# Start of a decoder kernel: order of the vector loads, of the first casts and of the passes of the first projection

## What is computed

```python
x = x + _L0_attn_ref(_layernorm(x, axis=-1), L0_attn_ln1_g, L0_attn_ln1_b,
                     L0_attn_Wq, L0_attn_bq, L0_attn_Wk, L0_attn_bk,
                     L0_attn_Wv, L0_attn_bv, L0_attn_Wg, L0_attn_bg, ...)
x = x + _L0_xattn_ref(_layernorm(x, axis=-1), ctx_1024, ...)
...
```

## Time and profile before

| | us |
|---|---|
| median of three runs | 1394.85 (1392.35 to 1399.29) |
| profiled execution, its own time | 1394.02 |
| its span | 1392.2 |
| PE, PEld, DVE, ACT, POOL busy in the span | 1247.0, 1071.0, 1004.3, 752.3, 251.1 |
| mean granted clock of PE | 0.963 |

### The profile page before, as it was taken

One profiled execution on the slowest core, in us unless ns is written; L12 is line 12 of the kernel. 1 busy time (PEld: TensorE's weight loads), 2 busy tenths in 40 slices (PEclk: granted clock), 3 DMA queues, 4 the chain that ended last, 5 costly groups with the idle time before them and its releaser, 6 DMA issues.

```text
span 1392.2 us, 27638 instructions
## 1 busy us (share of the span) xinstructions
PE 1247.0 (90%) x9826; PEld 1071.0 (77%) x9826; DVE 1004.3 (72%) x2479; ACT 752.3 (54%) x1781; POOL 251.1 (18%) x338
## 2 busy tenths in 40 slices
PE   5999999979999999999999999999888999979518
PEld 4889888868788777887778778787677777769518
DVE  5975776656667777777777777777777985676984
ACT  5653535335655555555555555555545764425862
POOL 2433333326000000000000000000034444110100
PEclk9999999989999999999999999999999999989859
DMA  9200101041000000000000000000020003310001
GB/s 286 67 1 5 43 1 46 0 155 48 1 12 12 12 13 11 0 12 11 12 11 11 1 11 12 11 0 1 1 61 2 3 2 114 103 30 0 1 0 48
DMA packets 34547, 40.65 MB, mean 29 GB/s; under 512 B 4889, under 2 KB 29066, under 8 KB 34442
## 3 DMA queue, kind: packets, MB, share of 16 engines
q1 hardware_dynamic: 33614, 39.24, 9.1%
q10 hardware_dynamic: 828, 0.14, 0.1%
HBM read 35.36 MB, written 4.01 MB: 28 GB/s over the span
## 4 chain that ended last, share of the span: by engine, by line
PE 50%; DVE 17%; issue 6%; ACT 4%; POOL 1%; DVEq 0%; DMA 0%; SPq 0%; ACTq 0%; POOLq 0%
PE bank L791 8%; PE bank L793 7%; PE bank L792 7%; PE bank L1014 4%; PE bank L1004 3%; PE bank L996 3%; PE bank L972 3%; ACT prob L1695 2%; DVE nmx L2375 2%; DVE amax L2574 2%; PE bank L1248 2%; DVE kTl L2146 2%; PE bank L1386 1%; PE bank L1266 1%; DVE prob L2392 1%
## 5 line engine op out<-in xcount | busy, mean ns | idle before, releaser
L1695 ACT ACTIVATE prob<-bank,nmx 100x361 f32<-100x361 f32 x256 | 142.5, 560 | 202.9 <-DVE nmx L2375 198.8
L2375 DVE TENSOR_REDUCE nmx<-bank 100x1 f32<-100x361 f32 x256 | 124.1, 526 | 62.6 <-PE bank L996 61.6
L695 POOL TENSOR_TENSOR frstd<-fmoments,eps 100x1 f32<-100x1 f32 x32 | 6.2, 194 | 645.0 <-DVE fmoments L2318 645.0
L791 PE MATMUL bank<-cxTh,wxkh 128*128 128x362 f32 x256 | 99.9, 390 | 9.3 <-DVE kTl L2146 8.2
L2392 DVE TENSOR_SCALAR prob<-prob,rsum 100x361 f32<-100x361 f32 x256 | 92.9, 405 | 4.5
L1004 PE MATMUL bank<-ident,prob 100*128 100x100 f32 (+1 forms) x768 | 89.6, 252 | 0.6 <-DVE prob L2392 0.5
L1004 PEld LDWEIGHTS bank<-ident,prob 100*128 100x128 f32 (+1 forms) x768 | 84.5, 151 | 6.2 <-DVE prob L2392 1.9
L791 PE MATMUL bank<-wxvh,cxTh 128*128 128x512 f32 (+1 forms) x192 | 84.4, 440 | 1.6 <-DVE vv L2298 1.2
L793 PE MATMUL bank<-cxTh,wxkl 128*128 128x362 f32 x256 | 84.1, 329 | 0.0
L792 PE MATMUL bank<-cxTl,wxkh 128*128 128x362 f32 x256 | 83.8, 327 | 0.0
L1014 PE MATMUL bank<-pT,vv 128*64 128x100 f32 (+1 forms) x1536 | 81.5, 255 | 1.7 <-ACT pT L1689 0.6
(11 more groups left out here) (432 smaller groups left out, 3703.6 us busy)
## 6 DMA issues: line engine op xcount, KB each, us to landing
cx<-in_ctx_dram SPq DMA_DIRECT2D x32, 128.0 KB, 2.1
xc<-in_ctx_dram SPq DMA_DIRECT2D x32, 128.0 KB
parked_weights<-parking SPq DMA_DIRECT2D x9, 256.0 KB, 5.6
mask_i<-in_mask_BxS_ik_dram SPq DMA_DIRECT2D x16, 141.0 KB
w<-in_L_attn_W_dram SPq DMA_DIRECT2D x2, 1024.0 KB, 13.5
cx<-in_ctx_dram SPq DMA_DIRECT2D x16, 105.0 KB, 2.0
xc<-in_ctx_dram SPq DMA_DIRECT2D x16, 105.0 KB
x<-in_x_dram SPq DMA_DIRECT2D x4, 400.0 KB
```

The costliest lines, as they stand in the source:

```text
L791: pe.matmul(o, wh, mh, start=start, stop=False)
L1695: nc.scalar.activation(prob[:, h % 4, :], bank[S_BANKS[e]][0:T, 0:S], ACT.Exp, bias=nmx[:, h:h + 1], accum_out=psum_[:, h:h + 1]).then_inc ...
L2375: nc.vector.tensor_reduce(nmx[:, h:h + 1], bank[S_BANKS[e]][0:T, 0:S], AX_X, ALU.max, negate=True).then_inc(xa_max, 1)
```

## The change

ACT no longer issues the last seven of the 15 vectors; SP does, right behind the first rows and ahead of the first weight. The four small tensors that are wanted late are issued by ACT after the two square roots, not before. A square root of one column (`warm`) is put right behind ACT's remaining issues, with no wait for the rows. The high parts of the first halves of Wk and Wg move from ACT to DVE (`tensor_copy`, followed by the subtraction), and DVE's waits for `l0_wh` drop by two. The low part of the rows for k = 1 of the first group moves from POOL to DVE, behind the low part of Wg. PE no longer waits for the low rows before `project(0)`: for K it runs the four passes without them as each k of the high rows is there, then waits for `l0_z` and runs the two passes with them.

```diff
--- before.py
+++ after.py
@@ -109,6 +109,7 @@
         decay = sb("decay", [P, KC])
         act_scale = sb("act_scale", [P, 4])
         pause = sb("pause", [1, 4])
+        warm = sb("warm", [P, 1])
         stats_all = sb("stats_all", [T, B, 6])
         moments_all = sb("moments_all", [T, B, 2])
         std_all = sb("std_all", [T, B])
@@ -383,6 +384,8 @@
         RELB_DMAS = 3 + 8
 
 
+        SP_VECTORS = 8
+
         def side_jobs():
 
             jobs = []
@@ -509,6 +512,11 @@
                 sp.dma_start(dst, a[name].rearrange("(k p) n -> p k n", p=P)).then_inc(count, 16)
 
             load_rows(0)
+            for name, n in VECTORS[SP_VECTORS:]:
+                r = COL[name]
+                src = (a[name].rearrange("(c h) d -> c (h d)", h=2) if name.startswith("L0_xattn")
+                       else a[name][0:n * P].rearrange("(c p) -> c p", p=P))
+                sp.dma_start(rows[r:r + n, :], src).then_inc(vec_in, 16)
             projections = (("L0_attn_Wk", wk0), ("L0_attn_Wg", wg0), ("L0_attn_Wv", wv0), ("L0_attn_Wq", wq0))
             for n, (name, dst) in enumerate(projections):
                 load_half(name, dst, 0, wa_in[n])
@@ -639,7 +647,7 @@
                 nc.gpsimd.tensor_tensor(el0[:, n % 2, :], full[:, n % 2, :], eh0[:, n % 2, :].bitcast(F32), ALU.subtract).then_inc(l0_es, 1)
 
             def rows_low0(g):
-                for k in range(KD):
+                for k in range(KD if g else 1):
                     pool.wait_ge(l0_y, KD * g + k + 1)
                     nc.gpsimd.tensor_tensor(rows_t[g % 2][1][:, k, :], y_rows[:, k, :], rows_t[g % 2][0][:, k, :].bitcast(F32), ALU.subtract).then_inc(l0_z, 1)
 
@@ -828,7 +836,7 @@
                 rows_h, rows_l = rows_t[n // KC % 2]
                 for kind in kinds:
                     high, low, b, free = KINDS[kind]
-                    if c == 0 and kind == 0:
+                    if c == 0 and kind == 0 and n:
                         pe.wait_ge(l0_z, KD * (n // KC) + KD)
                     if n == 0:
                         pe.wait_ge(l0_wl, kind + 1)
@@ -836,9 +844,18 @@
                         pe.wait_ge(l0_wb, kind + 1)
                     if n:
                         pe.wait_ge(free, n)
-                    for k in range(KD):
-                        mm = split_matmul(bank[b][:, 0:N], high[:, k, cols], low[:, k, cols], rows_h[:, k, :], rows_l[:, k, :],
-                                          k == 0, k == KD - 1)
+                    if n == 0 and kind == 0:
+                        for k in range(KD):
+                            pe.wait_ge(l0_y, k + 1)
+                            pe.matmul(bank[b][:, 0:N], high[:, k, cols], rows_h[:, k, :], start=(k == 0), stop=False)
+                            pe.matmul(bank[b][:, 0:N], low[:, k, cols], rows_h[:, k, :], start=False, stop=False)
+                        pe.wait_ge(l0_z, KD)
+                        for k in range(KD):
+                            mm = pe.matmul(bank[b][:, 0:N], high[:, k, cols], rows_l[:, k, :], start=False, stop=(k == KD - 1))
+                    else:
+                        for k in range(KD):
+                            mm = split_matmul(bank[b][:, 0:N], high[:, k, cols], low[:, k, cols], rows_h[:, k, :], rows_l[:, k, :],
+                                              k == 0, k == KD - 1)
                     mm.then_inc(l0_proj, 1)
 
             def summed(n, high, low, wh, wl, ready, count):
@@ -1469,19 +1486,14 @@
                 return vec[:, COL[name] + c:COL[name] + c + 1]
 
             act.dma_start(ident[:], a["identity"]).then_inc(vec_in, 16)
-            for name, n in VECTORS:
+            for name, n in VECTORS[:SP_VECTORS]:
                 r = COL[name]
                 src = (a[name].rearrange("(c h) d -> c (h d)", h=2) if name.startswith("L0_xattn")
                        else a[name][0:n * P].rearrange("(c p) -> c p", p=P))
                 act.dma_start(rows[r:r + n, :], src).then_inc(vec_in, 16)
             act.dma_start(logits[:], a["L0_attn_decay_logit"].rearrange("(c h) -> c h", h=2)).then_inc(vec_in, 16)
-            act.dma_start(delta[:, 0:KD * 8].rearrange("p (k n) -> p k n", k=KD),
-                          a["L0_ffn_delta_w"].rearrange("(k p) n -> p k n", p=P)).then_inc(small_in, 16)
-            act.dma_start(delta[:, KD * 8:], a["L0_ffn_delta_act"].partition_broadcast(P)).then_inc(small_in, 16)
-            act.dma_start(onehot[:], a["bucket_onehot"]).then_inc(small_in, 16)
-            act.dma_start(rel[0:BUCKETS, :], a["L1_attn_rel_emb"]).then_inc(small_in, 16)
-
             act.wait_ge(memsets, 2)
+            nc.scalar.activation(warm[:], eps[:], ACT.Sqrt)
             def rows_out(g, k, b):
                 nc.scalar.copy(zT[:, 2 * g:2 * g + 2, k, :], bank[b][:, 0:N].rearrange("d (a q) -> d a q", a=2)).then_inc(ln_done, 1)
 
@@ -1556,11 +1568,14 @@
                 nc.scalar.copy(cxTh[:, buf, k, 0:S], src[:, 0:S]).then_inc(xa_ch, 1)
 
             first_deviations(1, 0, 1)
+            act.dma_start(delta[:, 0:KD * 8].rearrange("p (k n) -> p k n", k=KD),
+                          a["L0_ffn_delta_w"].rearrange("(k p) n -> p k n", p=P)).then_inc(small_in, 16)
+            act.dma_start(delta[:, KD * 8:], a["L0_ffn_delta_act"].partition_broadcast(P)).then_inc(small_in, 16)
+            act.dma_start(onehot[:], a["bucket_onehot"]).then_inc(small_in, 16)
+            act.dma_start(rel[0:BUCKETS, :], a["L1_attn_rel_emb"]).then_inc(small_in, 16)
             act.wait_ge(prep_vec, 1)
             nc.scalar.mul(vecs[:], bank[SIDE_BANK0][:, 0:NV], DH ** -0.5)
             nc.scalar.copy(vec[:], bank[SIDE_BANK0][:, 0:NV]).then_inc(prep_done, 1)
-            weights_high(wa_in[0], 16, wk0h, wk0, slice(0, 512))
-            weights_high(wa_in[1], 16, wg0h, wg0, slice(0, 512))
             rows_high0(0)
             weights_high(wa_in[2], 16, wv0h, wv0, slice(0, 512))
             weights_high(wa_in[3], 16, wq0h, wq0, slice(0, 512))
@@ -2072,7 +2087,7 @@
 
             def weights_low(n, low, w, high, cols, done=l0_wl):
 
-                dve.wait_ge(l0_wh, n + 1)
+                dve.wait_ge(l0_wh, n - 1)
                 nc.vector.tensor_tensor(low[:, :, cols], w[:, :, cols], high[:, :, cols].bitcast(F32), ALU.subtract).then_inc(done, 1)
 
             def gated(n):
@@ -2184,7 +2199,16 @@
             both_deviations(1, 0, 1)
             rows_twice_normalized(0)
             for n, (low, w, high) in enumerate(((wk0l, wk0, wk0h), (wg0l, wg0, wg0h), (wv0l, wv0, wv0h), (wq0l, wq0, wq0h))):
-                weights_low(n, low, w, high, slice(0, 512))
+                if n < 2:
+                    cols = slice(0, 512)
+                    dve.wait_ge(wa_in[n], 16)
+                    link(nc.vector.tensor_copy(high[:, :, cols], w[:, :, cols]))
+                    rest(low[:, :, cols], w[:, :, cols], high[:, :, cols]).then_inc(l0_wl, 1)
+                else:
+                    weights_low(n, low, w, high, slice(0, 512))
+                if n == 1:
+                    dve.wait_ge(l0_y, KD)
+                    rest(rows_t[0][1][:, 1, :], y_rows[:, 1, :], rows_t[0][0][:, 1, :]).then_inc(l0_z, 1)
             dve.wait_ge(prep_done, 2)
             for g in range(NG):
                 first, follows = KC * g, g + 1 < NG
```

## The result

Over 20 runs of each, the changed kernel takes 1395.93 us (median; 1393.93 to 1400.85) against 1392.26 us (1388.55 to 1399.29): a ratio of 1.0028, with a 95% interval of 1.0017 to 1.0039. The change makes the kernel slower by 2.4 to 5.4 us. The start itself became nearly 4 us shorter; all of it, and more, is lost 20 us later.

What follows compares the result with a forecast made beforehand. The prediction took PE's side-job wait for L1_attn_W_attn to absorb the start's gain: 1394.0 with -4.1 + 4.1 + 1.0 (load delay) + 1.85 (half clock) - 0.26 (slack) = +2.6 gives 1396.6 us, range 1389.5 to 1401.

Steps and rivals of the forecast that it cites:

- The bound: Chain of waits reaches back only to 294.47 us; PE's timeline shows a 2.03 us wait for L1_attn_W_attn before `side_job(0)`.
- Roots and late loads: At the start on ACT: first root at 7.6 us, 2.55 sooner; PE's transposes of `u0` at 11.2, 2.15 sooner.
- Casts and low rows: Before the first projection: DVE copy 0.67 us, low rows 0.57 on DVE and 1.06 on POOL; G's passes 4.1 sooner.
- the likeliest case: Start's gain absorbed at PE's side-job wait, restart late and at half clock: 1396.6 us, chance 0.55.
- rival A: The start's gain gets through, needing L1_attn_W_attn at 30 us or a way past the side job: 1389.9 us, chance 0.13.
- Gain on arrival: PE comes to `side_job(0)` at 30.05 us, 4.1 sooner, and idles 7.1 us instead of 2.03.
- The delay of the load: Seven vector issues on SP ahead of the weights make L1_attn_W_attn land 1.0 us later, bounds 0 and 2.6.
- Half clock: PE restarts at the side job at half clock for 3.8 us, losing 1.85 us, bounds 0 and 3.6.
- What passes on: After the side job, `line` is 2.85 us late; ACT's slack of 0.26 leaves K and PE 2.6 us late.
- D: Early vectors or logits land late, `u0` transposes stay at 13.4 us, only the load's delay remains: 1394.8 us, chance 0.10.
- B: Three more of PE's 2 us stalls per group are followed by half clock, 5.1 us more: 1401.7 us, chance 0.08.
- C: Two of four PE stalls now followed by half clock are spared it, 3.4 us less: 1393.2 us, chance 0.14.

Runs made afterwards that it cites:

- e4: The changed kernel with 32 more matmuls on PE in front of the first side job, result unused: 1395.58 us, ratio 1.0029 to the kernel before.
- e6: The changed kernel run again unaltered, for a second profile: 1398.17 us, ratio 1.0032 to the kernel before.
- e5: The kernel before with only the last seven vectors moved to SP ahead of the weights: 1395.1 us, ratio 1.0020 to the kernel before.
- e1: The changed kernel with SP's loads of L1_attn_W_attn and L1_attn_W_proj issued ahead of W1 and W2: 1389.02 us, ratio 0.9984 to the kernel before.
- e10: The kernel before run again unaltered, for a second profile: ratio 1.0005 to the kernel before.
- e8: The changed kernel with the two L1_attn loads ahead of W1 and W2, run again: 1388.85 us, ratio 0.9971 to the kernel before.
- e3: The changed kernel with all 15 vectors issued by ACT as before: ratio 1.0025 to the kernel before.

## Why the prediction was right

It gave 1396.6 us and slower by 2.6; measured are 1395.93 us and 3.7 us more (2.4 to 5.4). That the time itself is off by 0.7 us only is in part luck: the sum began at 1394.0, 1.7 us above the median of 20 runs (1392.26), and was 1.1 us short in the difference.

**The bound.** The two views named were the right ones: a chain of waits that doesn't reach the start, and the wait in the earlier trace rows.

**Roots and late loads.** Predicted root 7.6, transposes 11.2; measured 7.34 and 10.55. The first rows landed 0.2 us sooner, and ACT issued the four loads from 8.28 us, beside the second root and not behind it, which I had added.

**Casts and low rows.** 0.69 us for the copy against 0.67. The low rows were mis-sized in the likeliest case: POOL and DVE took turns (2.10 and 1.41 us), which I had only given to rival A. That is most of why G's passes began 3.72 us sooner and not 4.1. By the Trainium skill, "SBUF — State Buffer", Who interferes with whom, a DVE operation with two SBUF sources excludes a GpSimd operation that reads SBUF; the rows of the changed kernel above agree. It should have changed nothing of the time, since it ends ahead of PE's wait; no run tests that alone.

**Gain on arrival.** PE came to the side job at 31.62 us, not 30.05: 2.5 us of gain arrived, not 4.1. The step I left out is the first rise of the clock. Work began 3.7 us sooner, but the clock rose only 1.7 us sooner (21.66 to 19.97), and half of the difference, 1.0 us, is lost. The idle time was therefore 5.83 us and not 7.1, with no effect on the end.

**The delay of the load.** 1.0 predicted, 1.27 in this pair of profiles, 2.0 in the second pair, 1.5 in the mean of eight: within its bounds of 0 and 2.6, and too small.

**Half clock.** 1.85 predicted. It held from 37.45 to about 40.2 us, 2.75 us, so 1.4; e4 puts its share in the hidden layer's start at 1.1. In this profile the term was 0.45 us too large, and the delay 0.27 too small. But half clock held for 4.4 us in e6 and for 5.0 in e5, 2.2 and 2.5 us lost: the term varies from 1.4 to 2.5, and 1.85 lies within.

**What passes on.** 0.26 us of slack in ACT's chain, as in the earlier trace rows: `line` late by 2.77, DVE waits 0.65 us for the root where it had waited for nothing, and K is late by 2.96, since DVE's first product took 0.83 us instead of 0.44. At the hidden layer 2.64 us: the sum's 2.6. That the two agree so closely is luck, since the second pair of profiles gives 4.8.

**The rivals.** A is excluded by the table; it came true in e1, where its condition, the load ahead of PE, was made to hold (1389.02 us, near its 1389.9). D is excluded by the start that did get shorter. What B and C count on, stalls that are followed by half clock or spared, does happen, as noise of both kernels: between 42 and 275 us, behind the side job, there are four such stretches in the kernel before and one in its second profile (e10), three in the changed kernel and two in its second (e6).

## What to carry over

Before making a start shorter, find the next point at which an engine waits for a transfer that nobody's progress speeds up, and ask what its queue holds ahead of it: here a shorter start paid only with the load moved ahead of ones that are wanted later. Issues put ahead of a busy stream can delay what is wanted 30 us later: seven small ones delayed this load by 1.5 us in the mean. And an engine that is first quick and then idle can be worse off than one that comes late: PE after 5.83 us of idle time restarted at half clock, after 2.03 us at full.

## What the runs showed of the hardware

PE's idle time and what follows: after 1.21, 1.84 and 2.03 us (e8, e10, before) the side job ran at full clock, after 3.92, 5.83 and 6.95 us (e5, changed, e6) at half clock, and after 4.39 us (e3) at full clock for its first 0.5 us and then at half. The length of the idle time alone doesn't decide it: in the kernel before, PE restarted at 109.13 us after 2.06 us of idle time at full clock, and the granted clock fell at about 110.4 us, while PE was at work, until 113.7. Half clock at the side job cost 1.4 to 2.5 us.

The first rise of the clock fell between 18.9 and 23.8 us over thirteen profiles and doesn't follow the start of the matmuls: of two profiles of one kernel, whose first passes were at 12.9 and 13.4, it came at 20.0 and 18.9. In two profiles each of one kernel (changed and e6, e1 and e8) it lay 1.1 and 1.6 us apart, half of which is lost or won.

A DVE copy of 128x1024 from float32 to float32r takes 0.69 us, a subtraction of that size 1.22; ACT's copy takes 1.06.
